# In the attention passes that also project a tile, TensorE takes two units at a time

## What is computed

```python
scores = jnp.einsum('bhtd,bhsd->bhts', xq, xk) * scale + bias[None]
attn = jax.nn.softmax(scores, axis=-1)
out = jnp.einsum('bhts,bhsd->bhtd', attn, xv)
out = out.transpose(0, 2, 1, 3).reshape(bsz, seqlen, N_HEADS * HEAD_DIM)
return out @ wo.T
```

## Time and profile before

| | us |
|---|---|
| median of 3 executions | 1277.71 |
| lowest, highest | 1276.04, 1278.7 |
| the profiled execution, by its device time | 1275.81 |
| its span in the trace | 1274.0 |

### The profile page before, as it was taken

One profiled execution on the slowest core, in us unless ns is written; L12 is line 12 of the kernel. 1 busy time (PEld: TensorE's weight loads), 2 busy tenths in 40 slices (PEclk: granted clock), 3 DMA queues, 4 the chain that ended last, 5 costly groups with the idle time before them and its releaser, 6 DMA issues.

```text
span 1274.0 us, 29144 instructions
## 1 busy us (share of the span) xinstructions
PE 1200.6 (94%) x9016; PEld 1014.3 (80%) x9016; DVE 912.8 (72%) x2386; ACT 751.3 (59%) x1629; POOL 385.1 (30%) x460
## 2 busy tenths in 40 slices
PE   6999999997999999999999999999988999999998
PEld 5778777785777788889888898889866788888876
DVE  5596776857999888788888888888854465636364
ACT  4545454553998887777777777777732244232230
POOL 1000000001589775453435444443521100202021
PEclk9999999998999999999999999999989999999999
DMA  4217262454676556454545454544443342101020
GB/s 166 100 75 264 105 238 120 190 200 180 206 253 237 179 179 199 156 169 149 180 157 188 143 183 158 178 158 161 152 158 124 116 157 66 66 34 66 34 67 34
DMA packets 99308, 189.36 MB, mean 149 GB/s; under 512 B 8080, under 2 KB 36880, under 8 KB 99216
## 3 DMA queue, kind: packets, MB, share of 16 engines
q1 hardware_dynamic: 99216, 188.21, 43.4%
HBM read 116.54 MB, written 71.63 MB: 148 GB/s over the span
## 4 chain that ended last, share of the span: by engine, by line
PE 80%; DVE 9%; issue 4%; DMA 3%; ACT 2%; POOL 1%; SPq 0%; DVEq 0%; ACTq 0%; POOLq 0%
PE bank L1422 18%; PE bank L1284 18%; PE bank L1357 13%; PE bank L1306 11%; PE bank L1315 10%; PE bank L1333 2%; PE bank L1332 2%; PE bank L1331 2%; PE bank L1346 2%; DVE inv_rms L1015 2%; DMA o_in<-o_scr 1%; DMA q_st<-q_scr 1%; DVE pT_lo L1068 1%; DVE raw L994 1%; DVE oT_lo L1080 1%
## 5 line engine op out<-in xcount | busy, mean ns | idle before, releaser
L836 ACT ACTIVATE p_sb<-u_sb,low 128x384 f32<-128x384 f32 (+2 forms) x512 | 274.4, 536 | 54.9 <-DVE low L1061 48.3
L1061 DVE CUSTOM_DVE_ANT_0 u_sb<-bank,bias 128x384 f32<-128x384 f32 (+2 forms) x512 | 231.6, 452 | 55.6 <-PE bank L1306 33.0
L1068 DVE TENSOR_TENSOR pT_lo<-bank,pT_hi 128x384 f16<-128x384 f32 (+2 forms) x512 | 232.3, 454 | 36.9 <-ACT pT_hi L843 21.3
L1306 PE MATMUL bank<-k_st,q_st 128*128 128x384 f32 (+2 forms) x1024 | 248.2, 324 | 6.8 <-DVE v_out L1035 2.9
L843 ACT ACTIVATE pT_hi<-bank 128x384 f16<-128x384 f32 (+2 forms) x512 | 206.7, 404 | 66.5 <-PE bank L1315 62.6
L1315 PE MATMUL bank<-ident,p_sb 128*128 128x128 f32 x1152 | 218.9, 281 | 21.4 <-DVE pT_lo L1068 14.7
L1306 PEld LDWEIGHTS bank<-k_st,q_st 128*128 128x128 f32 x1024 | 175.6, 191 | 31.4 <-DVE v_out L1035 3.3
L1315 PEld LDWEIGHTS bank<-ident,p_sb 128*128 128x128 f32 x1152 | 138.0, 141 | 59.9 <-ACT p_sb L836 40.4
L593 POOL TENSOR_TENSOR rstd<-var_eps,minus_half 128x1 f32<-128x1 f32 (+1 forms) x31 | 23.7, 766 | 475.1 <-DVE var_eps L943 469.3
L1332 PE MATMUL bank<-v_st,pT_hi 128*128 128x64 f16 x1152 | 158.5, 194 | 0.7 <-issue 0.7
L1331 PE MATMUL bank<-v_st,pT_hi 128*128 128x65 f16 x1152 | 158.2, 193 | 0.5 <-DVE pT_lo L1068 0.5
(11 more groups left out here) (121 smaller groups left out, 2329.3 us busy)
## 6 DMA issues: line engine op xcount, KB each, us to landing
q_scr<-qk SPq DMA_DIRECT2D x64, 512.0 KB, 2.7
q_st<-q_scr SPq DMA_DIRECT2D x32, 1024.0 KB, 7.7
k_st<-k_scr SPq DMA_DIRECT2D x64, 256.0 KB, 3.1
o_scr<-o_out SPq DMA_DIRECT2D x128, 128.0 KB, 2.5
o_in<-o_scr SPq DMA_DIRECT2D x16, 1024.0 KB, 5.2
k_scr<-qk SPq DMA_DIRECT2D x16, 512.0 KB, 2.9
z_in<-z_scr SPq DMA_DIRECT2D x8, 1024.0 KB, 6.7
v_scr<-v_out SPq DMA_DIRECT2D x4, 1040.0 KB, 5.7
```

The costliest lines, as they stand in the source:

```text
L836: nc.scalar.activation(p_sb[:, u % RING, 0:w], u_sb[:, u % RING, 0:w], ACT.Exp, scale=-1.0, bias=low[:, u % RING:u % RING + 1]).then_inc(p ...
L1061: nc.vector.tensor_tensor_reduce(out=u_sb[:, u % RING, 0:w], in0=bank[u % 2][:, 0:w], in1=bias[:, 2 * u // UNITS, u % REP, at:at + w], sca ...
L1068: nc.vector.tensor_tensor(pT_lo[:, u % RING, 0:w], bank[2 + u % 2][:, 0:w], pT_hi[:, u % RING, 0:w], ALU.subtract).then_inc(pT_ready, 1)
L1306: mm = nc.tensor.matmul(bank[u % 2][:, 0:w], q_st[:, s, r, P * i:P * i + P], k_st[:, s, part, P * key:P * key + w], start=(part == 0), sto ...
```

## The change

In the 11 passes with a projection TensorE now handles units in couples. At an even u, `couple_work` does the scores of u and u+1, then the transposes of u-2 and u-1, then the weighing of u-4 and u-3. At the odd u behind it, `project_unit` is called for both units: first `transpose_o` where it is due, then the two products of the one and the two of the other. The passes without a projection, and the programs of the other engines, stay as they are.

```diff
+            def couple_work(n, u):
+                one, other = ({stage: at for stage, *at in due(n, v)} for v in (u, u + 1))
+                for stage, work in (("scores", scores), ("transpose", transpose_p), ("weigh", weigh_values)):
+                    work(*one[stage])
+                    work(*other[stage])
+
+            def project_unit(tile, u):
+                m, at = divmod(u - START, STEP)
+                if m in range(4) and at == 0:
+                    transpose_o(tile, m)
+                m, at = divmod(u - START - 4, STEP)
+                if m in range(4):
...
+                    project_o(tile, m, (2 * at, 2 * at + 1), bank[7])
+
             def attend(n, tile=None):
                 for u in range(UNITS):
-                    unit_work(n, u)
-                    if tile is not None:
...
+                    if tile is None:
+                        unit_work(n, u)
+                    elif u % 2 == 0:
+                        couple_work(n, u)
+                    else:
+                        project_unit(tile, u - 1)
+                        project_unit(tile, u)
```

More of the change, by code:

```diff
@@ L1365, in unit_work @@
                         work(nn, uu)
+            def couple_work(n, u):
[9 more added lines that the diff above has]
+                if m in range(4):
+                    if m == 0 and at == 0:
+                        at_least(pe, y_normed, tile)
+                        if isinstance(tile, int):
+                            pe.wait_ge(wo_ready, QC)
+                    project_o(tile, m, (2 * at, 2 * at + 1), bank[7])
             def attend(n, tile=None):
                 for u in range(UNITS):
-                    unit_work(n, u)
-                    if tile is not None:
[L1371 to L1380, removed]
+                    if tile is None:
[5 more added lines that the diff above has]
+                        project_unit(tile, u)
             pe.wait_ge(v_ready, TT * B)
```

## The result

| | median us | lowest, highest | executions |
|---|---|---|---|
| before | 1276.61 | 1274.03, 1279.26 | 12 |
| changed | 1281.85 | 1279.95, 1284.01 | 12 |

The ratio of changed to before is 1.004, with a 95% interval from 1.0029 to 1.005: the change makes the kernel 5 us slower. I had forecast 2.6 us faster. In the two traces the last 11 passes, from the first scores of pass 5 to the last weighing of pass 15, take 6.3 us more (462.7 against 456.3), 0.55 us in a typical pass.

The account below looks back on a forecast made before the run. TensorE was taken to bound units 9 on, a chain through VectorE units 0 to 8; per pass -0.59 + 0.10 + 0.25 = -0.24 us, -2.6 over eleven passes, so median 1275.1 us (forecast 1271.5 to 1278.5, range 1267 to 1285).

## What to carry to other kernels

Batching steps on the busiest engine saves its switches, and delays everything that the other engines wait for by what now stands ahead: batch only where the busiest engine waits for none of them, and check by the starts of each stretch. Where it does wait, ask for which step of the other engine, and whether the new order makes it a later one. A full list on a second engine does not fix that engine's times: a delay at the point where it last waited is carried through it to the end. Filling that stood in a wait has to stay there, or the wait has to be moved first.

## What the hardware showed beyond that

After the 16-bit weighing, the next scores or product cost 0.085 us more, whichever it was (0.44 against 0.35, 0.31 against 0.23). Behind the transposes the same distances show and are given back by the last transpose, so only a comparison of whole couples tells a cost from a shifted start. And a head of the pass that leaves TensorE idle for a quarter of the time could bring the lower clock for 3.4 us. With couple (8,9) alone this lost 1.6 us in two of nine passes (8 and 11) and not in the other seven; it came once more in a kernel with the old order at the head, behind a wait for a DMA. What decides it stays open.
